# Ring offsets loaded ready-made, and one landing wait per batch of four, on the queue that copies gathered rows

## The reference

```python
k = _decomp(node_feat, node_type, w_comp_k, w_basis_k).reshape(n, H, DK)
...
kt = jnp.einsum('nhi,thij->tnhj', k, relation_att)[edge_type, src]
e = (q[dst] * kt).sum(-1) * relation_pri[edge_type] * scale
ex = jnp.exp(e - segment_max(e, dst)[dst])
a = ex / segment_sum(ex, dst)[dst]
vt = jnp.einsum('nhi,thij->tnhj', v, relation_msg)[edge_type, src]
agg = segment_sum(a[..., None] * vt, dst).reshape(n, DH)
out = relu(_decomp(agg, node_type, w_comp_a, w_basis_a) + node_feat @ loop_weight + bias)
return layernorm(x + out)
```

## Time and profile before

| | us |
|---|---|
| median of 3 runs | 1752.89 |
| lowest and highest of them | 1735.99, 1755.89 |
| the profiled execution, its own time | 1759.41 |
| span in its trace | 1757.2 |
| busy: TensorE / VectorE / GpSimd / ScalarE | 1160.7 / 986.6 / 881.5 / 785.6 |

### The profile page before, as it was taken

How to read it: one execution, slowest core, us unless ns; L and a number is a source line. 1 busy time by engine, 2 the same in 40 slices (tenths; PEclk the granted TensorE clock), 3 DMA queues, 4 the chain that set the end, 5 groups by cost and what they waited for, 6 DMA issues and landing times.

```text
span 1757.2 us, 31429 instructions
## 1 busy us (share of the span) xinstructions
PE 1160.7 (66%) x6730; PEld 962.9 (55%) x6730; DVE 986.6 (56%) x2832; ACT 785.6 (45%) x2217; POOL 881.5 (50%) x915
## 2 busy tenths in 40 slices
PE   8989875657556565566566655566565666656698
PEld 5445434656545554455455554565455565545587
DVE  7877463555445555445555554455554566545677
ACT  4667454444434434443344343443444354434324
POOL 2775354555555554545454545455545554545233
PEclk9999997777677767876777667766777687777699
DMA  8878754555555555545455555555555555555675
GB/s 261 323 289 316 284 172 140 157 148 158 152 159 153 157 151 151 149 141 151 150 163 148 158 152 154 148 160 164 151 162 154 154 168 148 155 150 162 187 242 194
DMA packets 225149, 309.08 MB, mean 176 GB/s; under 512 B 32423, under 2 KB 191119, under 8 KB 217781
## 3 DMA queue, kind: packets, MB, share of 16 engines
q1 hardware_dynamic: 159996, 188.75, 30.6%
q0 software_dynamic: 38880, 106.25, 23.4%
q10 hardware_dynamic: 26088, 12.08, 2.4%
HBM read 139.52 MB, written 58.78 MB: 113 GB/s over the span
## 4 chain that ended last, share of the span: by engine, by line
SPq 34%; issue 31%; PE 12%; DVE 9%; another core or an unknown queue 7%; DMA 2%; DVEq 2%; ACT 1%; POOL 1%; POOLq 0%; ACTq 0%
SPq L1173 27%; PE pb L1900 4%; SPq L1152 2%; PE pb L1923 2%; DVE agg L845 2%; SPq L481 2%; SPq L1170 2%; DVEq L814 2%; DMA kv<-ring 2%; PE pb L2084 1%; SPq L1168 1%; PE pb L2190 1%; PE pb L2028 1%; DVE kv L541 1%
## 5 line engine op out<-in xcount | busy, mean ns | idle before, releaser
L1458 POOL DMA_INDIRECT ring<-table,rows_idx x782 | 745.8, 954 | 736.6 <-SPq L1168 452.5
L2084 PE MATMUL pb<-work,onehot 128*128 128x136 f32 x1664 | 367.5, 358 | 214.1 <-DVE agg L845 152.8
L845 DVE TENSOR_TENSOR agg<-agg,pb 128x136 f32 x832 | 241.8, 291 | 459.9 <-remote 291.8
L2084 PEld LDWEIGHTS pb<-work,onehot 128*128 128x128 f32 x1664 | 307.0, 254 | 242.0 <-issue 210.9
L1650 ACT ACTIVATE work<-pb 128x512 f32<-128x512 f32 x208 | 124.0, 596 | 549.6 <-remote 376.2
L2028 PE MATMUL pb<-q_all,work 128*128 x1664 | 301.0, 340 | 1.3 <-issue 0.8
L2028 PEld LDWEIGHTS pb<-q_all,work 128*128 128x128 f32 x1664 | 280.6, 253 | 7.6 <-issue 4.9
L1637 ACT ACTIVATE work<-lane,neg_lane 128x128 f32<-128x128 f32 x800 | 253.3, 390 | 0.6
L2012 PE MATMUL pb<-ident,onehot 128*128 128x128 f32 x832 | 174.5, 347 | 115.6 <-issue 60.2
L2012 PEld LDWEIGHTS pb<-ident,onehot 128*128 128x128 f32 x832 | 125.4, 180 | 136.0 <-issue 71.3
L686 DVE TENSOR_TENSOR kv<-kv,pb 128x512 f32<-128x512 f32 x208 | 141.5, 680 | 96.6 <-issue 41.7
(11 more groups left out here) (239 smaller groups left out, 1237.2 us busy)
## 6 DMA issues: line engine op xcount, KB each, us to landing
kv<-ring SPq DMA_DIRECT2D x832, 128.0 KB
table<-kv SPq DMA_DIRECT2D x49, 1024.0 KB, 5.2
ring<-table,rows_idx POOLq DMA_INDIRECT x782
kv<-base_rows SPq DMA_DIRECT2D x7, 448.0 KB, 7.6
kv<-in_x_dram SPq DMA_DIRECT2D x8, 384.0 KB, 5.8
seg<-item_bias ACTq DMA_DIRECT2D x48, 64.0 KB
base_rows<-pair ACTq DMA_DIRECT2D x24, 128.0 KB
onehot<-coef_rows SPq DMA_DIRECT2D x3, 1024.0 KB, 5.5
```

The source lines that it names most:

```text
L845: v.tensor_tensor(a, a, PB[banks[i // 2 % len(banks)]][:, (i % 2) * 256:(i % 2) * 256 + W], ALU.add).then_inc(s_added, 1)
L1458: pool.indirect_dma_start(out=ring[:, o:o + 2 * D], out_offset=None, in_=table, in_offset=bass.IndirectOffsetOnAxis(ap=rows_idx[:, t:t + 1 ...
L2084: mm = t_.matmul(PB[banks[k % len(banks)]][:, u * 256:u * 256 + W], onehot[:, o:o + P], wv[:, b % WR, h * 2 + u, :], start=True, stop=True)
```

## The change

The part of `items` that makes the tile numbers also makes, for every item, the offset of its tile's slot in the ring, in elements: (tile modulo 16) times 256. It takes seven more VectorE instructions. `item_block` gets a third row, one more DMA on POOL's queue reads it back into a new partition of `band` (`iplace`), and the waits for these DMAs count to 64. In `bring`, SP loads four offsets and, with a second load, one tile number, that of the batch's fourth item. It waits once, before the first copy, until that tile has landed. The copies use the offsets as they are. The wait for the copies of the batch before and the addition to `s_freed` keep their place between the second and the third copy.

```diff
-        band = sb("band", [33, 3 * ITEMS // 2])
+        band = sb("band", [65, 3 * ITEMS // 2])
+        iplace = band[64:65, 0:ITEMS].bitcast(i32)
...
+                did(v.tensor_scalar(fc[:, 2, :], fc[:, 2, :], -1.0, None, ALU.add))
+                did(v.tensor_copy(ic[:, 3, :], fc[:, 2, :]))
+                did(v.tensor_scalar(ic[:, 3, :], ic[:, 3, :], RING.bit_length() - 1, None,
+                                    ALU.logical_shift_right))
+                did(v.tensor_copy(fc[:, 3, :], ic[:, 3, :]))
+                did(v.scalar_tensor_tensor(fc[:, 2, :], fc[:, 3, :], float(-RING), fc[:, 2, :],
+                                           ALU.mult, ALU.add))
+                did(v.tensor_scalar(fc[:, 2, :], fc[:, 2, :], float(2 * D), None, ALU.mult))
+                did(v.tensor_copy(ic[:, 3, :], fc[:, 2, :]))
...
-                each = tiles_of(4 * n, 4)
+                places = places_of(4 * n, 4)
+                landings = landings_of(4 * n)
                 after(sp, s_weighted, g - 2, NBATCH, b + 1)
                 for u in range(4):
                     if u == 2 and n > 0:
...
-                    if u % 2 == 0:
-                        sp.wait_ge(s_landed, each[u + 1] & 1023)
+                    if u == 0:
+                        sp.wait_ge(s_landed, landings[0] & 1023)
                         hold_apart(sp)
                     o = (par * G + b * 4 + u) * 2 * D
-                    sp.dma_start(kv[:, o:o + 2 * D],
-                                 ring[:, bass.ds(((each[u] - 1) & (RING - 1)) * (2 * D), 2 * D)])\
+                    sp.dma_start(kv[:, o:o + 2 * D], ring[:, bass.ds(places[u], 2 * D)])\
                         .then_inc(s_gathered[par][b], 16)
...
+            pool.dma_start(iplace[:, :], item_block[2:3, :]).then_inc(s_item_blocks, 16)
```

## The result

The changed kernel takes 1894.7 us (median of 4 runs) against 1751.9 us (median of 4), a ratio of 1.084 with a 95% interval of 1.075 to 1.094. In the experiments a median is over all runs of a kernel, while a ratio leaves out those more than 1.5% above the kernel's fastest. The spans of the two profiled executions differ by 135.0 us (1892.2 against 1757.2). Of these, 18.5 us are lost ahead of the first batch's products (they start at 266.3 us before, at 284.8 us after) and 117.7 us between the first product and the last (the loop: 1397.3 and 1515.0 us); behind the last product 1.2 us are won. "Loop" is the time from the start of the first product to the start of the last.

A forecast was written before the change was run, and what follows sets the result against it. The prediction took the consumers, working largely in POOL's quiet time, and not SP to bound the kernel. 1759.41 - 22 (waits for copies) + 1 (setup) gave 1738 us profiled, 1732 us as the runs' median; range 1660 to 1780.

The forecast's parts named there:

- SP isn't the limit; the consumers live on POOL's quiet time: Main loop: POOL's 452.5 us of waiting can't be had back, since VectorE works at 0.72 there, 0.28 to 0.46 during gathers.
- 22 instructions become 13: SP's train for a batch: 3.7 us becomes 3.34 in quiet time, 12.6 becomes 7.4 when held.
- held price of 0.57 us: SP while gathers are in flight: every instruction takes 0.57 us, whatever it is, from 18 instructions in 10.34 us.
- What L686 waits for copies is what can be won, 22 us: VectorE's products in the loop: their wait for SP's copies, at most 43.8 us, bounds the gain; the middle, 22 us, taken.
- with the same bursts of gathers: POOL's gathers in the loop: the gain assumed their bursts, and VectorE's busy share in them, unchanged.
- The quiet time would come back, forced by SP's wait for VectorE: Loop: a faster SP stands for VectorE, a hundred us or more, POOL stands at the full ring, and quiet time returns.
- Rival (c): POOL's gathers: faster freeing of slots makes bursts of four into eight, costing 48 us, 1801 us in all; chance 0.12.
- (b): POOL's gathers: bursts become shorter and VectorE works at 0.46 instead of 0.28, 48 us won, 1684 us; chance 0.18.
- One wait for the fourth tile, 0: SP's landing wait: waiting once for the fourth tile costs 0, up to 1.26 us in each of a few batches.
- Setup, 1.2 us: Ahead of the loop: seven more VectorE instructions of 0.17 us cost 1.2 us, the added DMA on POOL's queue 0.
- Rival (d): SP's train: the removed instructions are worth nothing, since the period follows the bursts as now; 1754 us; chance 0.14.

The follow-up runs named there:

- e3: The changed kernel with nine additions a batch to a semaphore nobody reads, on SP ahead of the copies; 1730.9 us, 0.995 of the kernel before.
- e12: The changed kernel with five additions a batch to a semaphore nobody reads, on SP ahead of the copies; 1733.2 us, 0.989 of the kernel before.
- e1: The changed kernel with its ready offsets, but SP waits for landings twice a batch as before and loads three tile numbers; 1813.0 us, 1.044.
- e2: The kernel before with its old register arithmetic, but only the one landing wait, for the fourth tile; 1766.0 us, 1.008.
- e4: The changed kernel, each SP batch from 12 on waiting for VectorE's products of the batch four before; 1832.1 us, 1.053 of the kernel before.
- e6: The changed kernel, each SP batch from 12 on waiting for VectorE's products of the batch two before; 1828.4 us, 1.051 of the kernel before.
- e11: The changed kernel, each SP batch from 12 on waiting for VectorE's products of the batch just before; 1830.5 us, 1.041 of the kernel before.
- e8: The kernel before with every second gather cut to 16 of its 128 rows, number of gathers and waits kept; 1749.6 us, 1.001.

## Why the prediction was wrong, by its steps

- *SP isn't the limit; the consumers live on POOL's quiet time.* Right. SP left the chain, and nothing was won by it. VectorE's share of quiet time, 0.72 in the sample, is 0.70 over both loops.
- *22 instructions become 13.* Right in number. When held, the first copy to the fourth now takes 5.9 us (median of 75 batches) in place of 7.3 (of 6 that lay wholly in held time); in quiet time 1.95 in place of 2.52. The held price of 0.57 us "whatever they are" was mis-read: between these two copies lie 15 instructions before and 7 after, which at 0.57 would be 8.6 and 4.0 us, and they took 0.49 and 0.84 us each (the earlier trace rows itself has 17 instructions up to its end, 0.61 us each). The loads were mis-sized: 0.80 and 0.44 us against 0.34 and at most 0.34, 0.56 us a batch. It didn't matter, as e3 and e12 show. The Trainium skill (Runtime: NRT & Kernel Launch, Instruction fetch mechanics) gives about 200 ns a register; the new load of four agrees with 0.80 us, the old one of four (0.30) and the new one of one register (0.44) don't; nor does e1's load of three (0.83).
- *What L686 waits for copies is what can be won, 22 us.* The wait did go (43.8 to 0.3 us; L686's idle time of every kind fell from 96.6 to 18.9), but none of it reached the end. The step that failed stands just ahead of it: "with the same bursts of gathers". It took the bursts, and VectorE's share in them, as given. The prediction named this as what would make it wrong; it should have been worked out, since SP's freeing is what starts and ends a burst. The share in held time fell from 403.2 / 936.9 = 0.43 to 305.6 / 919.8 = 0.33.
- *The quiet time would come back, forced by SP's wait for VectorE.* SP's wait came (229 us, where a hundred or more was said), and POOL's wait for SP didn't shrink but grew to 583.6 us.
- *Rival (c), runs of four become eight.* The right direction and the right mechanism as far as it goes, with 0.12 of the chances (its opposite, (b), had 0.18) and a third of the price. It counted a fifth of the time with gathers moved at 0.18, 35 us of VectorE's work and 48 of quiet time. Measured are 97.6 us of work and 139 of quiet time. Half of the work is what (c) priced, the longer runs (50 us); the other half, lower shares inside runs of either length, it didn't have. Its result of 1801 us lay outside the range; the chances that the range leaves out add up to 0.22 (0.06, a third of 0.18, 0.10) and not to 0.2.
- *One wait for the fourth tile, 0.* About 1% with the old train (e2, 1.008). With the short train the second wait and what goes with it are worth some 70 to 80 us (1.084 against 1.044 in e1). I take that for the price of instructions that slow SP and not of a wait, since five additions do more; no run tells the two apart.
- *Setup, 1.2 us.* 18.5 us were lost ahead of the first product, in part by 20 gathers in a row where there were 16. The step looked at VectorE's added work and not at SP's first batches.
- *Rival (d), the removed instructions are worth nothing.* It falls: their removal cost 143 us, and e12 adds five and takes away 162 us. The Trainium skill's rule on the recording block, that it holds back a producer rather than lose a record inside it (NOTIFIC — the notification-queue block, 7.1 Overflow), stays untested: every run on record carries a span, so it says nothing on the rule that the median moved about as the span did (142.8 and 135.0 us).

TensorE's own work isn't the cause: it is busy 1164.9 us after and 1160.7 before, at a mean granted clock of 0.764 and 0.783. The page's busy times of the changed kernel, all within 11 us of those before:

```profile
PE 1164.9 (62%) x6730; PEld 973.8 (51%) x6730; DVE 988.4 (52%) x2839; ACT 786.6 (42%) x2217; POOL 879.5 (46%) x916
```

**What stays open.** Why the shares inside the held time fell as well (0.58 to 0.55 in the first 4.5 us, 0.17 to 0.10 behind it), and with it why e4, e6 and e11 lose 4 to 5% with no more runs of eight than the kernel before. e6 has nearly the lengths of the kernel before (596 and 329 us against 593 and 344), and the 62 us of work that it lacks in held time are lower shares alone (0.54 and 0.06). So what is shown is that SP's shorter train, through POOL's rhythm, costs VectorE its work in held time; longer runs account for about half of that. Not tried was a slot ring of another size. Why TensorE's results are told late while POOL sends gathers was only bounded: it isn't the bytes (e8).

## What to carry to other kernels

A slow helper engine can be setting the rhythm of a resource that holds the others: before it is made faster, work out what its signals start, and what share of the work gets done in stretches of the new length. Here a helper that was held back a little was worth more than its instructions: 12 additions on POOL or 5 on SP won back 5 to 9% in the changed kernel. Held back too far (18 on SP, 32 on POOL) it became the limit. Measure the busy share against the time since the stretch began, not as one mean.

## What was unexpected in the hardware

- The hold doesn't follow the gathered bytes: 41% fewer of them (106.25 to 62.32 MB) left the time where it was (1.001). The packets fell by 16% only.
- A load of four registers on SP took 0.30 us (median) as the one load of a batch, from the strip, and 0.80 us as the first of two, from the new band. The second, from the same row of the strip as before, took 0.44 us for one register and 0.83 us for three (e1), so the place isn't the whole reason.
- An addition to a semaphore on POOL took 0.08 us from one to the next, but stood for some 0.7 us where it ran into a gather still being sent, so a pause of 12 additions was partly hidden and one of 32 added 3 us.
